# A hyperbolic transformer block on one core: the projection copy behind the repeats, the diagonals on ScalarE, half of a Gram block

## The reference

```python
ada = t_emb @ w_ada + b_ada                       # shifts, scales, gates of each sequence
xm = expmap0(layer_norm(logmap0(x)) * (1 + sc_msa) + sh_msa)
q, k, v = (_to_heads(plin(xm, w, b)) for w, b in ...)   # plin(x, w, b) = expmap0(logmap0(x) @ w + b)
attn = softmax(qt @ kt.T / sqrt(16))              # 16 heads of 16 features
attn_out = plin(_from_heads(expmap0(attn @ vt)), w_o, b_o)
x = mobius_add(x, expmap0(g_msa * logmap0(attn_out)))
xm = expmap0(layer_norm(logmap0(x)) * (1 + sc_mlp) + sh_mlp)
ff = plin(plin(xm, w_f1, b_f1), w_f2, b_f2)
y = mobius_add(x, expmap0(g_mlp * logmap0(ff)))
out = x_in + y
```

## Time and profile before

| | |
|---|---|
| median of 3 runs | 864.21 us (862.32 to 869.98) |
| the profiled execution | 866.16 us, of which the span of the trace is 864.4 us |
| start, up to the first `t` (L1118 at 54.86) | 55 us |
| attention slots | 55 to 564 us |
| statistics between the loops | 564 to 588 us |
| MLP slots | 588 to 861 us |
| busy in the span | PE 84%, DVE 79%, ACT 64%, POOL 47% |

### The profile page before, as it was taken

One profiled execution on the slowest core, in us unless ns is written; L12 is line 12 of the kernel. 1 busy time (PEld: TensorE's weight loads), 2 busy tenths in 40 slices (PEclk: granted clock), 3 DMA queues, 4 the chain that ended last, 5 costly groups with the idle time before them and its releaser, 6 DMA issues.

```text
span 864.4 us, 30460 instructions
## 1 busy us (share of the span) xinstructions
...
## 2 busy tenths in 40 slices
...
GB/s 325 350 67 51 57 55 45 50 50 55 55 50 48 48 55 55 55 48 45 53 55 55 54 42 19 17 61 82 125 86 146 135 124 134 147 100 146 134 62 86
DMA packets 51818, 74.04 MB, mean 86 GB/s; under 512 B 7081, under 2 KB 34609, under 8 KB 51762
## 3 DMA queue, kind: packets, MB, share of 16 engines
...
...
## 4 chain that ended last, share of the span: by engine, by line
PE 38%; DVE 23%; issue 19%; POOL 6%; DMA 4%; SPq 3%; DVEq 2%; ACT 2%; POOLq 0%; ACTq 0%
PE p_qkv L872 20%; PE p_oz L846 8%; DVE u L1134 7%; PE p_s L862 3%; SPq L348 3%; DVE g_all L1169 2%; DMA x_all<-in_x 2%; PE p_oz L840 2%; DMA mod<-mod_rows 2%; DVEq L50 1%; PE p_s L937 1%; DVE qk L1209 1%; DVE junk L1176 1%; DMA mod_b<-mod_rows 1%; POOL rt L483 1%
## 5 line engine op out<-in xcount | busy, mean ns | idle before, releaser
L872 PE MATMUL p_qkv<-wqkv,tT 128*128 128x256 f32 x768 | 194.7, 390 | 33.8 <-DVE u L1134 33.5
L872 PEld LDWEIGHTS p_qkv<-wqkv,tT 128*128 128x128 f32 x768 | 135.1, 192 | 64.9 <-DVE u L1134 25.3
L457 POOL TENSOR_TENSOR qk<-qk 128x512 f16<-128x512 f32 x64 | 73.9, 1155 | 146.0 <-ACT qk L604 146.0
L886 PEld LDWEIGHTS p_o<-v,pT 64*64 64x64 f32 x4096 | 68.9, 137 | 36.1 <-issue 36.1
L1162 DVE TENSOR_TENSOR z<-p_oz,bo 128x256 f32<-128x256 f32 x64 | 27.2, 425 | 78.8 <-PE p_oz L846 78.6
L609 ACT ACTIVATE qkT<-p_s 128x1024 f32<-128x1024 f32 x64 | 65.5, 1023 | 33.4 <-PE p_s L829 33.4
L886 PE MATMUL p_o<-v,pT 64*64 64x17 f32 x4096 | 73.4, 210 | 12.0 <-ACT pT L654 12.0
L654 ACT ACTIVATE pT<-p_s 128x1024 f32<-128x1024 f32 x64 | 65.5, 1023 | 20.6 <-PE p_s L862 20.6
L1134 DVE SCALAR_TENSOR_TENSOR u<-p_qkv,ct,bqkv 128x768 f32<-128x768 f32 x64 | 65.1, 1018 | 14.9 <-issue 12.9
L846 PE MATMUL p_oz<-wo,oT 128*128 128x256 f32 x256 | 75.2, 418 | 0.6 <-ACT oT L614 0.5
L829 PE MATMUL p_s<-ident,qk 128*128 128x128 f16 x1024 | 68.7, 221 | 6.5 <-issue 4.3
...
## 6 DMA issues: line engine op xcount, KB each, us to landing
mod<-mod_rows SPq DMA_DIRECT2D x128, 128.0 KB, 2.8
x_all<-in_x SPq DMA_DIRECT2D x8, 1024.0 KB, 14.3
gate<-mod_rows SPq DMA_DIRECT2D x128, 64.0 KB, 2.5
...
```

Of the source, the lines that this page charges most:

```text
L457: pool.tensor_tensor(low, qk[:, :].rearrange("p (a h d) -> p a h d", a=2, d=HD), qk4[:, :, :, 0, :], ALU.subtract).then_inc(low_ready, 1)
L872: mm = pe.matmul(p_qkv[:, a * D:a * D + D], tT[:, k, c, :], wqkv[:, c, a * D:a * D + D], start=c == 0, stop=c == C - 1)
L886: mm = pe.matmul(p_o[S * e:S * e + S, col:col + VW], pT[keys, e, g, :], v[keys, k, 2 * g + e, :], start=True, stop=True, skip_group_check= ...
```

## The change

1. **DVE's attention loop.** The slot is cut in two functions, `slot_until_rows` (`limit` to `sum_rows`) and `slot_from_bias` (from `add_bo` on). In the second one, `clip_t` and `project` stand directly behind `repeat_parts`, and `gate_z` and `dot_x` come after them; `project` of a tile is thus done at the end of a slot and no longer at the start of the next. The hardware loop begins at `add_bo` instead of at `project` (`run_slots_rotated`). POOL's `token_root` moves up by one slot (lag L_B instead of L_C).
2. **`split_ff_bias`** moves from slot 2 to slot 67 (`T + 3`), behind `dot_x`.
3. **The diagonals** are made by ACT, as four activations (Copy with a factor of each partition) between `evac_t2T` and `evac_out`, and no longer by POOL.
4. **Half the Gram block.** `wff` is laid out anew: [G00, W1W2, 2 G01] in part 0, and [nothing, W1W2, G11] in part 1. PE multiplies by 512 columns in part 0 and by 384 in part 1. The readers address the two Gram blocks as columns 0 to 127 and 384 to 511, and ACT makes eight copies at the start instead of seven.

```diff
+        def run_slots_rotated(eng, first_part, second_part, first, items, slots):
+
+            for s in range(first):
+                first_part(s // 2, s % 2)
+                second_part(s // 2, s % 2)
+            first_part(first // 2, 0)
+            with eng.Fori(first // 2, items // 2 - 1) as h:
+                second_part(h, 0)
+                first_part(h, 1)
+                second_part(h, 1)
+                first_part(h + 1, 0)
...
-                if on(h, off, L_C):
-                    token_root(2 * h + off - L_C, (off - L_C) % 2)
+                if on(h, off, L_B):
+                    token_root(2 * h + off - L_B, (off - L_B) % 2)
...
+                act.activation(wff[:, m, OUT_COLS], p_s[:, m * 512:m * 512 + D], ACT.Copy).then_inc(ffw_made, 1)
+                act.activation(wff[:, m, 3 * P * m:3 * P * m + P], s_bank[2 + m][:, m * P:m * P + P], ACT.Copy).then_inc(ffw_made, 1)
+            act.activation(wff[:, 0, 3 * P:4 * P], s_bank[2][:, P:2 * P], ACT.Copy, scale=2.0).then_inc(ffw_made, 1)
...
+            def diagonals(i, k, q, col, g):
+
+                act.wait_ge(al2_ready, g + 1)
+                act.wait_ge(be2_ready, g + 1)
+                after(act, out_psum, i - 1)
+                for j in range(2):
+                    for n, fac2 in enumerate((al2, be2)):
+                        act.activation(diags[k][j][n], ident[:, :], ACT.Copy, scale=fac2[:, q, col + j:col + j + 1]).then_inc(diag_ready, 1)
...
+                if on2(h, off, M_D):
+                    diagonals(slots - M_D, (off - M_D) % 2, parity(off, M_D), 2 * ((off - M_D) % GROUP),
+                              (TURN // GROUP) * h + (off - M_D) // GROUP)
                 if on2(h, off, M_O):
                     evac_out(slots - M_O, (off - M_O) % 2)
...
-                    mm = pe.matmul((p_qkv, p_s)[k][:, 512 * j:512 * j + 512], t2T[:, k, j, c, :], wff[:, c, :], start=False, stop=c == C - 1)
+                    mm = pe.matmul((p_qkv, p_s)[k][:, 512 * j + c * P:512 * j + 512], t2T[:, k, j, c, :], wff[:, c, c * P:2 * D],
+                                   start=False, stop=c == C - 1)
...
+            def slot_from_bias(h, off):
                 if on(h, off, L_L):
                     add_bo(2 * h + off - L_L)
                 if on(h, off, L_E):
                     repeat_parts(2 * h + off - L_E)
+                if on(h, off, L_C):
+                    clip_t(2 * h + off - L_C, (off - L_C) % 2)
+                    project(2 * h + off - L_C, (off - L_C) % 2)
                 if on(h, off, L_L):
                     gate_z(2 * h + off - L_L, (off - L_L) % 2, h + (off - L_L) // 2)
-                if on(h, off, L_C):
-                    clip_t(2 * h + off - L_C, (off - L_C) % 2)
                 if on(h, off, L_L):
                     dot_x(2 * h + off - L_L)
-
-            run_tiles(dve, slot)
+                if isinstance(h, int) and 2 * h + off == T + 3:
+                    split_ff_bias()
+
+            run_slots_rotated(dve, slot_until_rows, slot_from_bias, FIRST, T, T + L_L)
```

42 lines of the change are left out of this document (16 added, 26 removed).

## The result

The changed kernel takes 875.85 us (median of 4 executions, 875.71 to 876.83), the kernel before, beside it, 863.33 us (862.32 to 869.98). The ratio is 1.014, with a 95% interval of 1.011 to 1.018: slower by 1.4%, where 841 us was forecast.

A forecast was written before the change was run, and what follows sets the result against it. Attention was taken as bound by a ring of DVE's copy and PE's projection, the MLP as nearly full on DVE and PE. -22.6 + 1.7 - 2 + 0 - 1.5 = -24.4 on 866.2 gave 841.8, median 841 us, range 828 to 856.

The forecast's parts named there:

- The new place of the wait: Attention loop: PE's wait moves from DVE's copy to `o`, ahead of the projection's second part, 0.1 to 0.4 us.
- What the new neighbours expose: DVE's attention slot: new neighbours delay the end of `o` by 0.15 us (0.0 to 0.35), to 3.63 after `z`.
- The gain itself: Attention loop: slots fall from 7.68 to 7.29 us, 0.39 each over 58 slots, -22.6 us (-11 to -32).
- The loop's return under the wait ahead of `z`: DVE's attention loop: the return's 0.5 us are covered by DVE's wait of about 1 us ahead of `z`.
- My rival on the return: DVE's attention loop: a return of 3.0 us instead of 0.5 makes the kernel slower, 903 us; chance 0.04.
- ACT's cover: Attention slot: ACT's square waits for the later gate, `square_u` moves to about 4.2 us after `z`, within the cover.
- The split: Slot 67: the bias operations stand ahead of tile 62's softmax sums and delay the scores, +1.7 us (+1.0 to +2.2).
- The half Gram block: MLP stage: PE's product is 0.43 us shorter per pair, showing in the slots before the first output, -2 us.
- The diagonals: MLP loop: DVE's gain without POOL's disturbance is lost waiting for shifts and scales behind four activations (1.17 us), 0 us.
- if the rows did not bind: MLP loop: without DVE waiting for the shifts and scales, -12 us; part of the first rival, chance 0.27.
- The end: After the last factors: ACT makes diagonals quicker than POOL, POOL's root comes sooner, one product is shorter, -1.5 us.

The follow-up runs named there:

- e4: The changed kernel with PE's wait for `o` moved behind the projection's second part, directly ahead of the transpose of `o`: 853.1 us.
- e7: The kernel before, its order unchanged, with DVE's attention hardware loop beginning at `add_bo`: 856.6 us.
- e2: The changed kernel with DVE's 70 attention slots written out instead of in a hardware loop: 842.6 us.
- e3: The kernel before, in its old order, with DVE's 70 attention slots written out: 841.8 us.
- e16: e13 with the order of before (copy behind the dot product) in DVE's written-out attention slots: 828.0 us.
- e13: Changed kernel, DVE's attention written out, PE's `o` wait at its transpose, split in slot 2, diagonals behind `evac_out` except in MLP slots 32 to 40: 819.8 us.
- e8: The changed kernel with `gate_z` and `dot_x` moved behind `normalise`: 919.4 us.
- e1: The changed kernel without its first part: DVE's attention loop has the old order and loop start, POOL's earlier token root stays: 864.9 us.
- e9: The kernel before with the half Gram block alone: 860.9 us.
- e11: The changed kernel with the four diagonal activations behind `evac_out` instead of ahead of it: 880.0 us.
- e14: The changed kernel with DVE's attention loop over four slots instead of two: 875.1 us.
- e5: The changed kernel with `clip_t` moved from directly ahead of the copy to ahead of `z`: 860.7 us.

## Why the prediction was wrong, step by step

**The new place of the wait: right.** PE's wait for the copy fell from 33.5 us to 2.0, and one for `o` came in its place, ahead of the second part. That `o` then sets the pace was right as well; e4, which takes that wait away, shows it. The wait was to be 0.1 to 0.4 us and is 0.52 and 0.65.

**What the new neighbours expose: the step that failed.** I put `o` at 3.48 + 0.15 = 3.63 us after `z`, "with 0.0 and 0.35 as ends". Measured are 4.02 and 4.08: 0.54 and 0.60. The mean slot of 7.91 us (7.76 and 8.05) is 0.62 over the 7.29 forecast: the later `o` makes 0.42 of it, the stretch behind it, below, the rest.

Two things are in the 0.54 and 0.60. The base of 3.48 us was that of the first slot of the earlier trace rows alone: in the second, with the loop's return in it, `o` ends 4.12 us after `z`, and in e7, where the return is moved and the order is the old one, 3.60 and 3.73. The new neighbours then add 0.42 and 0.35 in the loop. Written out they add 0.11 (3.50 in e2, 3.39 in e3), and there my 0.15 would have done. What I priced at 0.15 and what the loop makes 0.42 of is for the most part the waits ahead of the copy. The piece of the order that stands ahead of the prediction holds a separate instruction with the waits for `ct_ready` and `qkv_psum` directly ahead of the copy. In the old order the dot product stood between `ct` and that instruction and covered it. In the new one nothing does: 0.31 to 0.32 us, in each loop slot, and 0.09 in the written-out ones.

The trace of before could have warned me. The dot product starts 0.36 us ahead of the copy in the first slot of the earlier trace rows and 0.91 ahead in the second:

```profile
301.34 0.43 DVE L1176 SCALAR_TENSOR_TENSOR junk<-x_all,g_all 128x256 bf16 x1
...
308.77 0.42 DVE L1176 SCALAR_TENSOR_TENSOR junk<-x_all,g_all 128x256 bf16 x1
```

I called the 0.48 us of "issue" in the second "the loop's return" and, as the first shows no gap, took it that the body costs nothing else. The sequencer's instructions in that trace say otherwise: the branch starts at 308.90, the next instruction at 309.21, and from there to the copy at 309.68 stand the waits for `ct_ready` (309.33) and for the rest, which in the first slot start at 301.41 and run under the dot product. The return put them 0.5 us later, behind the dot product: 0.35 of the 0.48 us are the copy's own waits with nothing to cover them.

**The gain itself: a wrong base.** I took 0.39 us a slot as what the order would give, from 7.68 to 7.29. The 7.29 were met, but only in e2, where the slots are written out (7.29), and by chance: in its shorter slot the pieces were 3.50 + 0.06 + 3.69 instead of 3.63 + 0.12 + 3.54. The last term, from PE's second part to the next `z`, was 0.15 us too short in every slot and 0.30 in the one ahead of the return. And the old order, written out, takes 7.30 (e3), so in this kernel as it stands the 0.39 us were nearly all the price of the loop and its return, and not one that the new order could win back. In e3 `ct` starts 1.16 to 1.19 us after `z`, as before; only the copy comes earlier, 1.63 us after `z` where it was 1.73, and 1.64 where it was 2.30. PE's waits of 0.41 and 0.68 us thus become 0.31 and nothing: the second was the loop's altogether. The first is mostly that of the order; taking it away gained nothing, since in e2 the wait for `o` comes in its place (0.21), and it was worth 0.19 us a slot only where that wait stood at the transpose (e16 against e13). The written-out slots of the kernel before hinted at it in the same trace: the first full one, ahead of the loop, takes 7.31 us from `z` to `z` (85.34 to 92.65).

**The loop's return under the wait ahead of `z`: half right.** It gave 0.12 us a slot and not 0.27 (e7). DVE waits for PE there about 1 us, but the wait for `z_psum` is one of the separate instructions at the head of the loop: in the trace of the change it starts at 320.54, when PE lets it, another wait at 320.62 and `z` only at 320.69, while the `z` of the slot ahead (312.64) has no such instruction in front. So the `z` that follows the return comes 0.15 us later than the others (8.05 = 4.08 + 0.13 + 3.84, the other slot 4.02 + 0.05 + 3.69). My rival on the return had the right sign and the wrong mechanism, and its deciding size of 1.6 us was never near.

**ACT's cover: right in the change, thin.** Its wait for the gated vector became 1.55 us in that slot and delayed no one who sets the pace; `square_u` starts 4.35 us after `z`, where I had about 4.2. e8 moved the gate 1.7 us further, and the kernel takes 919 us.

**The split: +1.4 us, forecast +1.7.** In e1 the `z` behind it comes 8.84 us after the one ahead, in the kernel before 7.42, with the granted clock at 0.50 in both. In the changed kernel PE stands there for `o`:

```profile
565.63 0.69 PE L859 MATMUL p_oz<-ident,o 128*128 128x128 f32 x2 [3.35 <-DVE o L1174]
```

**The half Gram block: right.** Forecast -2, measured -1.7 in the first 16 pairs of the change, and -2 in the median alone (e9).

**The diagonals: right in each piece.** The four activations take 1.17 us to the start of the next instruction, the very number of the forecast:

```profile
719.64 0.39 ACT L746 ACTIVATE oT<-ident,al 128x128 f32<-128x128 f32 x1
719.93 0.39 ACT L746 ACTIVATE oT<-ident,be 128x128 f32<-128x128 f32 x1
720.23 0.39 ACT L746 ACTIVATE bqkv<-ident,al 128x128 f32<-128x128 f32 x1
720.52 0.39 ACT L746 ACTIVATE bqkv<-ident,be 128x128 f32<-128x128 f32 x1
720.81 0.58 ACT L751 ACTIVATE x_all<-p_o 128x512 f32 x1
```

The Trainium skill (ScalarE: Activation LUTs, "What ACT_TABLE_LOAD costs") gave 293 ns from one start to the next as an estimate; the rows show 290 to 300, so the trace agrees. DVE's `scale_t2` is back at 480 ns, as in the earlier trace rows, and what that gave is waited for again:

```profile
DVE lnx L1285 <- DMA mod_b<-mod_rows: 10.8, 9, 2.1
DVE lnx L1285 <- DMA mod<-mod_rows: 7.9, 6, 2.1
DVE ct L1357 <- issue: 4.1, 1, 4.1
```

(Waits of DVE from 650 to 850 us: total, times, longest. Before it was 6.3 us for `mod` and 1.0 for `mod_b`.) That is 3.1 us a group where I had written 3.7. Of the 12 us that I said would come "if the rows did not bind", 7.7 came in e11 from the first to the last `ct`, up to 1.6 us a group, and were lost again in the drain, a place to which I hadn't followed the move. The return of the MLP loop cost 4.1 us in this trace instead of 3.0, a term that I didn't have; with the same MLP code it is 3.0 in e1, 3.1 in e14 and 4.3 in e5, and why it varies stays open. I also wrote that PE released both starts of `evac_out` in the earlier trace rows; it released the copy directly ahead of each, which comes to the same 7.41 us.

**The end: -1.8 us, forecast -1.5.** Right.

The other terms of the sum were within 2 us of what came. The one that failed was counted 58 times over, and the upper end of its range, 0.35 us, rested on no row; the range of the whole hung on it.

**What stays open.** e2 and e14 show that the cost in the new order belongs to the loop body and hardly to the return, and e5 that 0.32 us of it hang on the wait for `ct`. The times of the sequencer's instructions say where these 0.32 us go; how the rest of the 0.5 to 0.7 us of a slot divides among register arithmetic and waits against registers isn't told apart by a run, nor whether a written-out program is faster for the constants alone or also for how it is fetched.
